# One shared row buffer in a five-layer graph kernel: the first gathers of a sweep issued in the phase before it

## The reference

```python
h = relu(layernorm(x)); x = x + gine(h)       # sum over edges of relu(h[src] + edge_attr_64 @ We + be), MLP, batch norm
h = relu(layernorm(x)); x = x + sage(h)       # mean over edges of h[src], concat, linear, relu
h = relu(layernorm(x)); x = x + gatv2_ffn(h)  # 8 heads, softmax over the edges of a destination, then an FFN with gelu
h = relu(layernorm(x)); x = x + gat(gat(h))   # two attention layers, 4 heads and 1 head, elu behind each
```

## Time and profile before

| | |
|---|---|
| median of three runs | 7460.23 us |
| span of the profiled execution, first to last instruction | 5796.6 us |
| median less span: what lies around it | 1663.6 us |
| POOL busy | 3988.9 us (69%), 4207 instructions |
| PE busy | 4596.1 us (79%) |
| DVE, ACT busy | 2702.8 us, 1216.6 us |
| TensorE clock granted, mean | 0.779 |
| first and last gather start of sweeps 0 to 4 | 60.4 to 1104.1; 1195.7 to 2233.7; 2282.0 to 3349.0; 3621.1 to 4659.7; 4710.4 to 5750.5 us |

### The profile page before, as it was taken

One profiled execution on the slowest core, in us unless ns is written; L12 is line 12 of the kernel. 1 busy time (PEld: TensorE's weight loads), 2 busy tenths in 40 slices (PEclk: granted clock), 3 DMA queues, 4 the chain that ended last, 5 costly groups with the idle time before them and its releaser, 6 DMA issues. The chain is left out here.

```text
span 5796.6 us, 89863 instructions
## 1 busy us (share of the span) xinstructions
PE 4596.1 (79%) x21959; PEld 3153.3 (54%) x21959; DVE 2702.8 (47%) x8105; ACT 1216.6 (21%) x3182; POOL 3988.9 (69%) x4207
## 2 busy tenths in 40 slices
PE   5888888657777776999999977687777758887887
PEld 4777777535556564444444433455555535555555
DVE  4222222321111113677777766555555545555555
ACT  2111111221211211222222258111111111111111
POOL 6777777457777775777777700777777747777775
PEclk9999999975555555999999989666666666666665
DMA  5333333244444443555555510455555534444443
GB/s 151 106 105 105 105 104 104 74 150 106 112 114 107 118 114 90 160 165 165 165 165 164 166 38 24 109 114 114 113 114 115 113 77 107 111 109 110 109 111 78
DMA packets 559823, 663.58 MB, mean 114 GB/s; under 512 B 196431, under 2 KB 390909, under 8 KB 558717
## 3 DMA queue, kind: packets, MB, share of 16 engines
q1 hardware_dynamic: 424909, 382.99, 22.2%
q0 software_dynamic: 134640, 277.80, 21.1%
HBM read 580.95 MB, written 86.19 MB: 115 GB/s over the span
## 5 line engine op out<-in xcount | busy, mean ns | idle before, releaser
L1792 POOL DMA_INDIRECT soft_rows<-table,sources x2496 | 2388.6, 957 | 1128.2 <-issue 737.7
L1422 POOL DMA_INDIRECT sum_rows<-table,sources x832 | 785.7, 944 | 343.9 <-issue 249.6
L1088 POOL DMA_INDIRECT term_rows<-table,sources x832 | 791.4, 951 | 289.4 <-issue 289.4
L1923 PE MATMUL psum<-soft_onehot,soft_message 128*128 128x64 f32 x3328 | 647.6, 358 | 107.1 <-DVE soft_message L2066 105.0
L1923 PEld LDWEIGHTS psum<-soft_onehot,soft_message 128*128 128x128 f32 x3328 | 586.1, 266 | 188.0 <-issue 181.8
L1119 PE MATMUL psum<-term_onehot,term_term 128*128 128x64 f32 x1664 | 403.9, 425 | 188.5 <-DVE sums L1171 176.6
L1464 PE MATMUL psum<-sum_onehot,sum_rows 128*128 128x64 f32 x1664 | 360.4, 391 | 222.7 <-DMA sum_rows<-table,sources 218.4
L1119 PEld LDWEIGHTS psum<-term_onehot,term_term 128*128 128x128 f32 x1664 | 370.7, 328 | 242.1 <-issue 242.0
L1165 DVE TENSOR_TENSOR term_term<-psum,term_rows 128x512 f32<-128x512 f32 x208 | 143.9, 692 | 753.0 <-issue 349.0
L1464 PEld LDWEIGHTS psum<-sum_onehot,sum_rows 128*128 128x128 f32 x1664 | 343.5, 304 | 278.0 <-issue 273.8
L1919 PEld LDWEIGHTS psum<-soft_onehot,soft_weights 128*4 128x4 f32 (+1 forms) x3328 | 284.9, 109 | 305.9 <-issue 293.0
(11 more groups left out here) (277 smaller groups left out, 6619.9 us busy)
## 6 DMA issues: line engine op xcount, KB each, us to landing
soft_onehotT<-onehotsT SPq DMA_DIRECT2D x312, 256.0 KB
soft_onehot<-onehots SPq DMA_DIRECT2D x624, 128.0 KB, 2.1
soft_attrs<-in_ea128T SPq DMA_DIRECT2D x208, 256.0 KB
soft_rows<-table,sources POOLq DMA_INDIRECT x2496
term_attrs<-in_ea64T SPq DMA_DIRECT2D x208, 128.0 KB, 2.8
onehots<-term_onehot SPq DMA_DIRECT2D x208, 128.0 KB
sum_onehot<-onehots SPq DMA_DIRECT2D x208, 128.0 KB, 2.7
onehotsT<-sum_flat SPq DMA_DIRECT2D x208, 128.0 KB
```

Of the source, the lines that this page charges most:

```text
L1088: pool.indirect_dma_start(rows[:, k, t, :], None, io.table0[0:NCH * CN], bass.IndirectOffsetOnAxis(sb.sources[:, g * TPG + t:g * TPG + t + ...
L1422: pool.indirect_dma_start(rows[:, k, t, :], None, io.table1[0:NCH * CN], bass.IndirectOffsetOnAxis(sb.sources[:, g * TPG + t:g * TPG + t + ...
L1792: pool.indirect_dma_start(rows[:, k, t, :], None, table[0:NCH * CN], bass.IndirectOffsetOnAxis(sb.sources[:, g * TPG + t:g * TPG + t + 1], ...
L1923: last = pe.matmul(bank[:, 0:W], message[:, g.slot(4), b, :], onehot[:, k, b], start=b == 0, stop=b == TPG - 1)
```

## The change

All sweeps use one ring in one buffer, allocated once for all phases. Group 0 of sweeps 1 to 4 is gathered by POOL in the block of the phase before: in `norm1_phase` and `ffn_phase` in a POOL block that is new, in `sum_sweep` and `soft_sweep` 3 behind the sweep's own last gather. It waits only for the stores of the table. The other store of each chunk counts on a new semaphore, `beside`, which SP waits for as before. The `gathered` semaphores belong to the new class and are allocated before the phase in which their first gathers are issued. The last tile of a sweep, whose indices are all padding, is gathered with 16 indices instead of 128.

Since the ring stays allocated, three other buffers moved: the two large ones of `ffn_phase` (`gelu`, `h`) into the part of the ring behind group 0, and `degree_in` of `sum_sweep` into `sb.rel_group`, which is no longer needed there.

```diff
+class Ahead:
+    def __init__(self, nc, sb, ring, phase, table, width):
+        self.sb, self.ring, self.table = sb, ring, table[0:NCH * CN]
+        self.rows = ring[:, 0:AROUND * TPG * width].rearrange("p (k t f) -> p k t f", k=AROUND, t=TPG)
+        self.gathered = [nc.alloc_semaphore(f"{phase}_gathered{k}") for k in range(AROUND)]
+    def beyond(self, first, shape):
+        _, a, b, n = shape
+        return self.ring[:, first:first + a * b * n].rearrange("p (a b n) -> p a b n", a=a, b=b)
+    def gather(self, pool, g):
+        k = g % AROUND
+        for t in range(TPG):
+            real = slice(0, P if (g * TPG + t) * P < E else 16)
+            pool.indirect_dma_start(self.rows[real, k, t, :], None, self.table,
+                                    bass.IndirectOffsetOnAxis(self.sb.sources[real, g * TPG + t:g * TPG + t + 1], 0)).then_inc(self.gathered[k], 16)
 def narrow_layers(nc, io, sb):
+    with ExitStack() as ctx:
+        ring = ctx.enter_context(nc.sbuf_tensor("ring", [P, AROUND * TPG * (D + 4)], F32))[:]
+        to0 = Ahead(nc, sb, ring, "term0", io.table0, D)
+        term_sweep(nc, io, sb, to0)
+        to1 = Ahead(nc, sb, ring, "sum1", io.table1, D + 1)
+        norm1_phase(nc, io, sb, "norm1", to1)
+        to2 = Ahead(nc, sb, ring, "soft2", io.table2, D)
+        sum_sweep(nc, io, sb, to1, to2)
+        soft_sweep(nc, io, sb, 2, to2, None)
+        to3 = Ahead(nc, sb, ring, "soft3", io.table3, D + 4)
+        ffn_phase(nc, io, sb, "ffn", to3)
+        to4 = Ahead(nc, sb, ring, "soft4", io.table4, D + 1)
+        soft_sweep(nc, io, sb, 3, to3, to4)
+        soft_sweep(nc, io, sb, 4, to4, None)
...
@@ MeanNodes (GatNodes, ffn_phase alike)
-        sp.dma_start(chunk_rows(io.xr_table, c), self.rows[:, k, :, D:2 * D]).then_inc(s.stored[k], 16)
+        sp.dma_start(chunk_rows(io.xr_table, c), self.rows[:, k, :, D:2 * D]).then_inc(s.beside[k], 16)
+    def table_stored(self, eng):
+        eng.wait_ge(self.s.stored[0], 16 * (NCH - NCH // 2))
+        eng.wait_ge(self.s.stored[1], 16 * (NCH // 2))
...
@@ rows_out of MeanNodes (GatNodes, ffn_phase alike)
-        freed(v, s.stored, c, 32)
+        freed(v, s.stored, c, 16)
+        freed(v, s.beside, c, 16)
...
@@ sum_sweep (soft_sweep alike, with s.message, and with the last two lines only where `ahead` is given)
-                for g in range(G):
-                    k = g % AROUND
+                for g in range(1, G):
                     if g >= AROUND:
                         pool.wait_ge(s.scattered, g + 1 - AROUND)
-                    for t in range(TPG):
-                        pool.indirect_dma_start(rows[:, k, t, :], None, io.table1[0:NCH * CN], ...
+                    of.gather(pool, g)
+                nodes.table_stored(pool)
+                ahead.gather(pool, 0)
...
@@ norm1_phase (ffn_phase alike)
+            @block.gpsimd
+            def _(pool):
+                if ahead:
+                    pool.wait_ge(s.stored[0], 16 * (CH - CH // 2))
+                    pool.wait_ge(s.stored[1], 16 * (CH // 2))
+                    ahead.gather(pool, 0)
...
@@ each sweep
-    phase_end(nc, tuple(s) + tuple(nodes.s))
+    phase_end(nc, tuple(s) + tuple(nodes.s) + (gathered,))
```

More of the change, by code:

```diff
@@ L1048, in tile @@
             return ctx.enter_context(nc.sbuf_tensor(f"{phase}_{name}", shape, dt))[:]
-        rows = tile("rows", [P, AROUND, TPG, D])
+        rows, gathered = of.rows, of.gathered
         onehot = tile("onehot", [P, 8, TPG, W])
@@ L1371, in tile @@
             return ctx.enter_context(nc.sbuf_tensor(f"{phase}_{name}", shape, dt))[:]
-        rows = tile("rows", [P, AROUND, TPG, D + 1])
+        rows, gathered = of.rows, of.gathered
         onehot = tile("onehot", [P, AROUND, TPG, W])
@@ L1523, in __init__ @@
         self.s = sems(nc, f"nodes{layer}", staged=2, node_major=2, den=2, inverse=2, ratio=2, biased=2, low=2, relu=2, exp=2,
-                      elu=2, out=2, eluT_psum=2, eluT=2, proj=2, rows=2, stored=2)
+                      elu=2, out=2, eluT_psum=2, eluT=2, proj=2, rows=2, stored=2, beside=2)
         self.sum_in = tile("sum_in", [P, 2, CN])
@@ L1672, in tile @@
             return ctx.enter_context(nc.sbuf_tensor(f"{phase}_{name}", shape, dt))[:]
-        rows = tile("rows", [P, AROUND, TPG, width])
+        rows, gathered = of.rows, of.gathered
         onehot = tile("onehot", [P, 4, TPG, W])
@@ L1786, in _ @@
             def _(pool):
-                for g in range(G):
-                    k = g % AROUND
+                for g in range(1, G):
                     if g >= AROUND:
                         pool.wait_ge(s.message, g + 1 - AROUND)
-                    for t in range(TPG):
-                        pool.indirect_dma_start(rows[:, k, t, :], None, table[0:NCH * CN],
-                                                bass.IndirectOffsetOnAxis(sb.sources[:, g * TPG + t:g * TPG + t + 1], 0)).then_inc(s.gathered[k], 16)
+                    of.gather(pool, g)
+                if ahead:
+                    nodes.table_stored(pool)
+                    ahead.gather(pool, 0)
             @block.scalar
```

89 lines of the change are left out of this document (49 added, 40 removed).

## The result

Changed kernel: 7477.0 us (median of 13 runs, 7460.9 to 7499.4); kernel before beside it on the same chip: 7458.85 us (13 runs). Ratio 1.0026, 95% interval [1.0014, 1.0037]: slower by 0.26%, 18 us. The prediction was 7488.8 us, in a range of 7470 to 7505.

The account below looks back on a forecast made before the run. POOL's gather stream was taken to bound sweeps 0, 1, 3 and 4, the other engines' start sweep 2. Seams 33.6, last tile -6, clears +1 gave +28.6 us on 7460.2: 7488.8 us, range 7470 to 7505.

Parts of the forecast that it names:

- 1663.6 us lie around the span, in which no instruction of the kernel runs: Whole run: the timed median exceeds the profiled span by 1663.6 us outside the kernel's instructions, added unchanged to the sum.
- POOL the bound: Sweeps 0, 1, 3 and 4: POOL's gather stream, 5.0 us a group, sets the time.
- The drain: At the four seams: POOL's drain before the barrier ends 8.6 us behind the last gather ahead.
- 2.6 + 14.1: Each FFN or sweep seam: 2.6 us for the table store's landing, 14.1 us for POOL's wake, four gathers and drain.
- rival 1: At the seams: the drain behind four gathers is short, under some 1 us; -5.4 us, 7454.8 us; chance 0.16.
- it depends neither on the kind of DMA nor on how many are queued: POOL's drain at phase ends: the 8.6 us tail is the same whatever DMAs went before.
- The agreement of the three rows: Drains of the first phase and the layer 1 and layer 3 sweeps each end 8.6 us behind POOL's last DMA.
- In sweeps 1, 3 and 4 POOL's: POOL's lateness, 8.9, 7.7 and 6.8 us, reaches these sweeps' ends; with sweep 2's 10.2 us, 33.6 us.
- Rival 2: All four sweeps follow the other engines' start: seams cost 51.5 us, in all +46.5, 7506.7 us; chance 0.10.
- rival 3: At four seams the first group's 5 us vanish and the barrier isn't held: -26 us, 7434 us; chance 0.04.
- The last tile: End of four sweeps that end on POOL: 16 indices instead of 128 save 1.5 us each, -6 us.
- The clears: Up to five phase ends: clearing two semaphore ranges instead of one costs 0 to 2 us, taken as +1.

Follow-up runs that it names:

- experiment 1: The kernel before, unchanged, timed and profiled a second time: 7465.7 us, ratio 0.9988.
- Experiment 7: The changed kernel with one more POOL drain behind the last gather of sweeps 1 and 3, before the table-store wait: 7557.29 us, ratio 1.0005 to the kernel before.
- experiment 4: The changed kernel with four groups gathered ahead at each seam instead of one: 7481.68 us, ratio 1.0017 to the kernel before.
- 9: The kernel of Experiment 7 with POOL held to 8 groups ahead in sweeps 0, 1, 3 and 4: 5806.01 us, ratio 1.0008 to the kernel before.
- 10: The kernel before with POOL held to 8 groups ahead in sweeps 0, 1, 3 and 4: 5805.02 us, ratio 1.0005.
- experiment 8: The changed kernel with POOL allowed 8 groups ahead instead of 16 in all sweeps: 7652.0 us, ratio 1.0117 to the kernel before.
- Experiment 2: The kernel before with only the last tile of each sweep cut to 16 indices: 7465.66 us, ratio 0.9998.
- experiment 3: The changed kernel with no group gathered ahead, all groups behind the barrier: 7474.59 us, ratio 1.0002 to the kernel before.
- experiment 12: The kernel of 9 with sweep 2 also starting at 8 groups ahead, one more every 5 groups up to 16: 7376.9 us, ratio 0.9894 to the kernel before.

## Why the prediction was right, and what in it was wrong

- **"1663.6 us lie around the span, in which no instruction of the kernel runs": wrong.** 2.2 us do (experiment 1). The timed executions are of another kind, in which the sweeps take 23 to 38% longer. All that was read of sweeps in the quick trace (5.0 us a group, POOL the bound) did not hold for what was timed: there a group takes 5.8 (sweep 0) to 7.0 us (sweep 2), and POOL's waits for DVE in the softmax sweeps are 1134.9 us in place of the 22.3 of the earlier trace rows. That the seams are nearly as long in both kinds saved the sum, and that was luck: nothing in the prediction asked which kind the trace was of.
- **The drain: right at two seams, wrong at two.** 8.6 us at the ends of sweeps 1 and 3, as forecast (table store to barrier 16.0 and 15.8 us; forecast 2.6 + 14.1 = 16.7). At the ends of norm1 and ffn it was 1.7 us, which is nearly rival 1's case (under some 1 us). The step that failed is "it depends neither on the kind of DMA nor on how many are queued". It depends on how many gathers POOL has issued since its last drain. In every profile, quick or long, with idle time in between or not, it ends 8.9 us behind the last gather after 836 gathers, 8.6 after 832, 8.2 after 828 and 7.25 after 816, alike to 0.01 us for each count; 1.7 to 1.9 us after 4 and 2.3 after 16. From 816 to 836 that is 0.08 us for each gather, which does not reach down to nothing (832 x 0.08 = 67 us), so the law in between is open. Experiment 7 shows that it is a drain that starts the count again. The agreement of the three rows was half luck: the two sweeps had 832 gathers each, and the setup's 8.6 us is no fixed number. In the fourteen profiles it lies between 8.3 and 10.3 us; these are the drain and the last small DMAs of experiment 1, 34.7 - 24.4 = 10.3 us:

```profile
L390 POOLq DRAIN  x1: 14719/14719/14719, 20.0 to 20.0; - x1
```
```profile
23.25 1.15 POOL L434 DMA_DIRECT2D L_b<-in_L_b  x2
```

  Why 43 small DMAs leave a drain as long as 832 gathers do is open.
- **"In sweeps 1, 3 and 4 POOL's" lateness reaches the end: right in sum.** Forecast were 8.9, 8.1, 7.7 and 6.8 us. Counted from the last table store to the first gather behind the barrier (one group further on than before) and less one group's 5.0 us where before had it still to gather, the changed kernel is later by 1.6, 8.0, 0.4 and 6.0 us, 16.0 in all, against a measured 15 (profiles) to 18 us (times). The mis-sized terms are norm1 and ffn. Rival 2 (all engines' start, +46.5) is refuted by the result and by experiment 4; rival 3 (-26 us) by the result. The mechanism, POOL's stream as what sets the end of a sweep, is borne out in the quick kind, where 9 and 10 are 1 us apart with barriers 22.8 us later. In the long kind, which was timed, POOL waits for the others within the sweeps, and that the same reckoning gives the right sum there is not explained: it may be luck. Why a group ahead is given back in the long kind is open; experiment 8 suggests that it shortens the burst, and was not made to show it.
- **The last tile, -6 us: too large.** Experiment 2: -1.5 us, from -12 to +9 by its interval, and 0.09 us of POOL's time. The rule of the Trainium skill in "DMA: Bandwidth & Descriptors" (Anatomy of one DMA — SWDGE path), a fixed cost for each such DMA whatever its size, was the better guide: by it the tile gives nothing. The trace agrees in direction for the part that POOL's record covers, 0.86 against 0.95 us, an eighth of the indices at nine tenths of the time.
- **The clears, +1:** 11 more, of 0.16 us (median). With the split semaphores and the moved buffers 0.02% [-0.09, +0.14] (experiment 3). Nothing speaks against the term; no time resolves 1 us.

So +28.6 became +18: two of four drains were short (less 2 x 6.9 = 14 us), and the tile brought nothing (plus 6), which gives +21. The two errors have opposite signs.

## What to carry to other kernels

Before any sum, compare the profile's span with the timed median; where they differ as here (5796.6 against 7460.2 us), look whether the trace is of another kind of execution, for a bound read from it must be read again in one of the timed kind. Work moved ahead of a barrier brings its engine's drain with it: put a drain where that engine idles anyway, and the one at the barrier becomes short. Three drains that agree prove no constant when two of them stand behind equally many gathers. A prefetch ring that is filled in one burst can hold up those who read it; fill it gradually, and check per phase, since one phase may need the full depth.

## What the runs showed that was not expected

- One kernel has two times, by the batch (each batch ran on one chip): 5803 us in one, 7459, 7468, 7552 and 7468 us in four others. POOL, DVE and ACT are busy equally long in both, within 0.6%. In the long kind, SP's queue moved 0.68 MB in the 60 us from 80 to 140 us of sweep 0 and POOL's 3.15 MB; in the quick kind 3.02 and 3.18. The lines are the DMA queues' (packets, MB, share of 16 engines), long kind first:

```profile
q0 software_dynamic: 1534, 3.15, 18.7%
q1 hardware_dynamic: 601, 0.68, 3.4%
```
```profile
q0 software_dynamic: 1544, 3.18, 21.9%
q1 hardware_dynamic: 2554, 3.02, 15.0%
```

  So the gathers' packets move as fast, and it is their readers that stand still. In the long kind SP's sequencer also pauses with nothing to wait for (847 times in experiment 1, 903 times and 651 us in the changed kernel), which it never does in the quick traces of the kernel before and of experiment 9. Later in the sweeps the engines wait for SP's loads: in 300 us of the changed kernel's sweep 4 (6900 to 7200 us) DVE waits 69.5 us for the one-hot rows, and POOL 82.6 us for DVE. Whether SP's pauses are the cause or come with it, no run shows; what differs stays open.
- A POOL DRAIN ends 1.7 to 1.9 us behind the last of 4 gathers, 2.3 behind the last of 16, and 7.25, 8.2, 8.6 and 8.9 behind the last of 816, 828, 832 and 836 since the last drain; idle time before it changes nothing.
- The steady pace of sweep 0 in the long kind did not depend on the ring, as that of sweep 2 did: from group 32 to 207 of sweep 0 it is 5.8 us a group with 16 groups in flight (changed kernel) and 5.9 us with 8 (experiment 12). What sets it is open.
